# A fused attention and ternary FFN layer on one core: h split one slot later, output scaling on GpSimd, score maxima ahead of gate and up, and weight pieces shared out anew

## What is computed

```python
qkv = x @ Wqkv + bqkv                     # 16 heads of 16, 4 key/value groups
scores = einsum('bqhd,bkhd->bhqk', q, k) / HD
out = softmax(scores) @ v                 # then @ Wout + bout
x = layernorm(x + attention(x))
w_hat = clip(round(w / scale), -1, 1) * scale   # per 64 weights, scale = mean|w|, in bf16
gate, up = split(x @ ternary(w_gate_up).T)      # 1024 each
h = silu(gate) * up
x = layernorm(x + rms_norm(h) @ ternary(w_proj).T)
```

## Time and profile before

| | |
|---|---|
| median of 3 runs | 626.21 us (624.43 to 627.9) |
| the profiled execution: its time, its span | 624.11 us, 622.1 us |
| PE, DVE, ACT, POOL busy | 90%, 74%, 60%, 46% |
| one batch in the loop | 33.3 us |

### The profile page before, as it was taken

How to read it: one execution, slowest core, us unless ns; L and a number is a source line. 1 busy time by engine, 2 the same in 40 slices (tenths; PEclk the granted TensorE clock), 3 DMA queues, 4 the chain that set the end, 5 groups by cost and what they waited for, 6 DMA issues and landing times.

```text
span 622.1 us, 14146 instructions
## 1 busy us (share of the span) xinstructions
PE 556.9 (90%) x4368; PEld 465.6 (75%) x4368; DVE 457.7 (74%) x1066; ACT 373.6 (60%) x738; POOL 288.7 (46%) x404
## 2 busy tenths in 40 slices
PE   5668989999999999999899999999999999899772
PEld 4656768788788787878787877778787877777762
DVE  7785875777877878787878787877878787755753
ACT  4454645666666666757566666666666756575442
POOL 5432331353536353535435453536354535455763
PEclk9697999999999999999999999999999999999996
DMA  7963354444352517061624344352617070101001
GB/s 232 153 131 44 79 86 95 71 95 69 78 104 69 113 45 138 23 136 25 146 35 115 65 98 80 77 102 61 118 43 136 17 144 5 36 3 35 18 0 35
DMA packets 53932, 49.08 MB, mean 79 GB/s; under 512 B 6144, under 2 KB 53888, under 8 KB 53888
## 3 DMA queue, kind: packets, MB, share of 16 engines
q1 hardware_dynamic: 51152, 47.60, 37.1%
q10 hardware_dynamic: 2736, 0.92, 0.6%
HBM read 33.29 MB, written 14.68 MB: 77 GB/s over the span
## 4 chain that ended last, share of the span: by engine, by line
PE 56%; DVE 25%; issue 9%; POOL 4%; ACT 3%; ACTq 2%; DMA 1%; DVEq 0%; POOLq 0%; SPq 0%
PE ffn_ps L447 13%; PE short_ps L447 10%; PE pv_ps L544 8%; PE short_ps L494 6%; PE exp_ps L503 5%; PE down_ps L529 5%; DVE row_max L776 5%; PE short_ps L552 4%; DVE w_hat L809 3%; DVE gated L817 3%; DVE x L880 2%; DVE st L898 2%; DVE h_f L824 2%; DVE r L895 2%; ACTq L746 2%
## 5 line engine op out<-in xcount | busy, mean ns | idle before, releaser
L776 DVE TENSOR_REDUCE row_max<-short_ps 128x2 f32<-128x512 f32 x256 | 173.7, 682 | 47.5 <-PE short_ps L494 47.4
L933 POOL TENSOR_TENSOR h_lo<-h_f,h_hi 128x256 fp32r<-128x256 f32 x128 | 94.8, 740 | 237.5 <-ACT h_hi L672 227.0
L690 ACT ACTIVATE probs<-exp_ps 128x1024 f32<-128x1024 f32 x128 | 130.9, 1023 | 32.7 <-PE exp_ps L503 30.7
L447 PE MATMUL ffn_ps<-x1T_hi,wguT 128*128 128x256 f32 x480 | 125.6, 295 | 21.0 <-DVE x1T_lo L765 10.7
L494 PE MATMUL short_ps<-k_st,q_st 65*128 65x256 f32 x512 | 116.4, 309 | 12.8 <-DVE row_max L776 12.4
L447 PE MATMUL ffn_ps<-x1T_lo,wguT 128*128 128x256 f32 x480 | 118.8, 281 | 0.0
L447 PEld LDWEIGHTS ffn_ps<-x1T_hi,wguT 128*128 128x128 f32 x480 | 90.4, 188 | 30.5 <-DVE h_f L824 13.9
L681 ACT ACTIVATE tanh<-ffn_ps 128x256 f32<-128x256 f32 x120 | 45.8, 381 | 104.3 <-PE ffn_ps L447 83.3
L494 PEld LDWEIGHTS short_ps<-k_st,q_st 65*128 65x128 f32 x512 | 82.1, 192 | 23.7 <-DVE row_max L776 12.3
L447 PEld LDWEIGHTS ffn_ps<-x1T_lo,wguT 128*128 128x128 f32 x480 | 90.5, 189 | 0.0
L938 POOL TENSOR_TENSOR sq_sum<-sq_sum,h_sq 128x256 f32<-128x256 f32 x112 | 82.9, 741 | 0.0
(11 more groups left out here) (98 smaller groups left out, 864.6 us busy)
## 6 DMA issues: line engine op xcount, KB each, us to landing
q_st<-q_dram SPq DMA_DIRECT2D x128, 128.0 KB, 4.1
q_dram<-q_p SPq DMA_DIRECT2D x16, 512.0 KB, 3.0
xn<-in_L_attn_x_dram SPq DMA_DIRECT2D x16, 256.0 KB, 4.6
k_st<-k_dram SPq DMA_DIRECT2D x64, 64.0 KB, 2.3
res<-in_L_attn_x_dram SPq DMA_DIRECT2D x16, 256.0 KB, 3.3
out_dram<-y_out SPq DMA_DIRECT2D x16, 256.0 KB, 2.2
wgu_raw<-in_L_ffn_w_gate_up_dram SPq DMA_DIRECT2D x8, 256.0 KB, 6.5
k_dram<-k_p SPq DMA_DIRECT2D x16, 128.0 KB, 3.1
```

The costliest lines, as they stand in the source:

```text
L447: last = pe.matmul(dst, a, b, start=start and i == 0, stop=stop and i == len(pairs) - 1)
L690: act.activation(probs[:, st.s % 4], exp_ps[:], ACT.Exp).then_inc(exp_done, 1)
L776: dve.tensor_reduce(row_max[:, st.par, head * TT:(head + 1) * TT], short(n, f"max{i}")[:].rearrange("p (t k) -> p t k", t=TT), AX.X, ALU.m ...
L933: pool.tensor_tensor(h_p[1][:, st.s % 4, :], h_f[:, st.s % 2, :], h_p[0][:, st.s % 4, :].bitcast(F32), ALU.subtract).then_inc(h_lo, 1)
```

## The change

Seven edits.

- On PE `gate_up` is issued behind `max_scores(…, 0)` and `exp_scores`, no longer ahead of them. On ACT `exp` goes ahead of `tanh` and of the copy of x.
- `h_hi`, `h_sq` and `h_lo` of a slot's `h_f` are issued one slot later (H_HIGH0, H_LOW0 from 31 to 32), and the sum of squares, its mean and the inverse root move from slot 7 to slot 0 (SUM_SQ, MEAN_SQ, INV from 39 to 40).
- BANK_TABLE changes in slots 0, 1 and 7.
- LN2_APPLY (y_out, two instructions a batch) moves from DVE to POOL.
- `keep_clock` ends at t = 16 and not at 29.
- Pieces 4 to 11 of the weights have their two multiplications on POOL, so that POOL does four instructions for such a piece; `w_hat` has four buffers and not two, `w_scale` two.
- The turns of the pieces follow a table: pieces 1, 2 and 3 are turned at t = 8, 9 and 10, before at 6, 7 and 9; the others as before.

```diff
-SUM_SQ = 39
+SUM_SQ = 40
-H_HIGH0 = 31
-H_LOW0 = 31
-MEAN_SQ = 39
-INV = 39
+H_HIGH0 = 32
+H_LOW0 = 32
+MEAN_SQ = 40
+INV = 40
...
-BANK_TABLE = {0: {"max0": 1, "pv1": 0, "max1": 2},
-              1: {"max0": 1, "x": 2, "max1": 0, "shift1": 1},
+BANK_TABLE = {0: {"max0": 2, "pv1": 0, "max1": 1, "sq": 2},
+              1: {"max0": 1, "x": 0, "max1": 2, "shift1": 1},
...
-              7: {"max0": 2, "v": 0, "max1": 1, "sq": 2}}
+              7: {"max0": 2, "v": 0, "max1": 1}}
...
-W_MAKE, W_TURN, W_PLACE = 1, 4, 5
+W_MAKE = 1
+W_TURN = (5, 8, 9, 10, 12, 14, 16, 18, 20, 22, 24, 26)
-CLOCK_FROM, CLOCK_TO = 2, 30
+CLOCK_FROM, CLOCK_TO = 2, 17
+W_POOL_FROM = 4
...
         @block.tensor
             def slot(n):
-                if st := n.chunk(FFN0):
-                    gate_up(n, st)
                 if st := n.chunk(MAX0):
...
                     exp_scores(st)
                 keep_clock(n, 2)
+                if st := n.chunk(FFN0):
+                    gate_up(n, st)
...
         @block.scalar
             def slot(n):
+                if st := n.chunk(EXP0):
+                    wait(act, exp_scored, st.count(8, st.s + 1))
+                    wait(act, pv_done, st.count(4, st.s // 2 - 1))
+                    act.activation(probs[:, st.s % 4], exp_ps[:], ACT.Exp).then_inc(exp_done, 1)
                 if st := n.chunk(FFN0):
...
-                if st := n.chunk(EXP0):
-                    wait(act, exp_scored, st.count(8, st.s + 1))
...
         @block.vector
+                dve.tensor_tensor(hat, w_abs[:, c % 2], half, ALU.is_gt).then_inc(w_dve, 1)
+                if c < W_POOL_FROM:
+                    dve.wait_ge(w_dve, 3 * c + 1)
+                    dve.tensor_tensor(hat, hat, scale, ALU.mult).then_inc(w_dve, 1)
+                    dve.wait_ge(w_dve, 3 * c + 2)
+                    dve.tensor_tensor(hat, hat, w_sign[:, c % 2], ALU.mult).then_inc(w_dve, 1)
...
-                if st := n.once(LN2_APPLY):
-                    wait(dve, rstd2_done, st.count(1, 1))
...
         @block.gpsimd
+                if st := n.once(LN2_APPLY):
+                    wait(pool, rstd2_done, st.count(1, 1))
+                    wait(pool, stored[st.par], st.count2(16, 0))
...
+                    if c >= W_POOL_FROM:
...
+                        pool.tensor_tensor(hat, hat, scale, ALU.mult).then_inc(w_pool, 1)
+                        pool.wait_ge(w_pool, w_pool_count(c) + 1)
+                        pool.tensor_tensor(hat, hat, w_sign[:, c % 2], ALU.mult).then_inc(w_pool, 1)
```

More of the change, by code:

```diff
@@ L220, in postln_layer @@
         w_sign = sb("w_sign", [P, 2, PG, Q_GROUP], BF16)
-        w_hat = sb("w_hat", [P, 2, PG, Q_GROUP], BF16)
+        w_hat = sb("w_hat", [P, 4, PG, Q_GROUP], BF16)
         w_sum = sb("w_sum", [P, PG])
-        w_scale = sb("w_scale", [P, PG], BF16)
+        w_scale = sb("w_scale", [P, 2, PG], BF16)
         w_half = sb("w_half", [P, PG], BF16)
@@ L359, in piece, with turned_piece, w_dve_count, w_pool_count @@
             return W_READ.index(n.t - later) if n.it is None and n.t - later in W_READ else None
+        def turned_piece(n, later):
+            return W_TURN.index(n.t - later) if n.it is None and n.t - later in W_TURN else None
+        def w_dve_count(c):
+            return 3 * min(c, W_POOL_FROM) + max(c - W_POOL_FROM, 0)
+        def w_pool_count(c):
+            return 2 * min(c, W_POOL_FROM) + 4 * max(c - W_POOL_FROM, 0)
         block = ctx.enter_context(nc.Block())
@@ L563, in keep_clock @@
                     return
-                turned = sum(at + W_TURN < n.t for at in W_READ)
+                turned = sum(at < n.t for at in W_TURN)
                 if turned:
@@ L633, in slot @@
                     turn(bank, [att[:, t, m * P:(m + 1) * P] for m in range(DT) for t in range(TT)], att_turned)
-                if (c := piece(n, W_TURN)) is not None:
+                if (c := turned_piece(n, 0)) is not None:
                     turn_weights(c)
@@ L748, in slot @@
                                 .bitcast(F32), shift_p[half][part][:].bitcast(F32)).then_inc(shift_loaded[half], 16)
-                if (c := piece(n, W_PLACE)) is not None:
+                if (c := turned_piece(n, 1)) is not None:
                     act.wait_ge(w_tr, c + 1)
@@ L794, in tern_weights @@
                 dve.wait_ge(w_red, 3 * c + 1)
-                dve.tensor_scalar(w_scale[:], w_sum[:], 1.0 / Q_GROUP, 1e-8, ALU.mult, ALU.max).then_inc(w_red, 1)
+                dve.tensor_scalar(w_scale[:, c % 2], w_sum[:], 1.0 / Q_GROUP, 1e-8, ALU.mult, ALU.max).then_inc(w_red, 1)
                 dve.wait_ge(w_red, 3 * c + 2)
-                dve.tensor_scalar(w_half[:], w_scale[:], 0.5, None, ALU.mult).then_inc(w_red, 1)
+                dve.tensor_scalar(w_half[:], w_scale[:, c % 2], 0.5, None, ALU.mult).then_inc(w_red, 1)
                 dve.wait_ge(w_red, 3 * c + 3)
-                if c >= 2:
-                    dve.wait_ge(w_tr, c - 1)
+                if c >= 4:
+                    dve.wait_ge(w_tr, c - 3)
                 half = w_half[:].unsqueeze(2).broadcast_to([P, PG, Q_GROUP])
[L802 to L809, removed]
+                scale = w_scale[:, c % 2].unsqueeze(2).broadcast_to([P, PG, Q_GROUP])
+                hat = w_hat[:, c % 4]
+                dve.tensor_tensor(hat, w_abs[:, c % 2], half, ALU.is_gt).then_inc(w_dve, 1)
[4 more added lines that the diff above has]
+                    dve.tensor_tensor(hat, hat, w_sign[:, c % 2], ALU.mult).then_inc(w_dve, 1)
             def slot(n):
@@ L834, in slot @@
                     wait(dve, y_copied, st.count(1, 1))
+                    wait(dve, y_done, st.count(TT, 0))
                     for t in range(TT):
@@ L939, in slot @@
                                            ).then_inc(h_summed, 1)
+                if st := n.once(LN2_APPLY):
+                    wait(pool, rstd2_done, st.count(1, 1))
+                    wait(pool, stored[st.par], st.count2(16, 0))
+                    pool.sem_inc(pool_waited, 1)
+                    for t in range(TT):
+                        pool.tensor_scalar(y_out[:, st.par, t, :], r2[:, t, :], mv2[:, t, 0:1], rstd2[:, t:t + 1],
+                                          ALU.subtract, ALU.mult).then_inc(y_done, 1)
                 if st := n.once(RSTD1):
```

18 lines of the change are left out of this document (9 added, 9 removed).

## The result

| | before | changed |
|---|---|---|
| median | 625.32 us (4 runs, 623.56 to 627.9) | 648.65 us (4 runs, 646.64 to 651.3) |
| ratio | | 1.0372, interval 1.0318 to 1.0427 |
| profiled execution, span | 622.1 | 646.4 |

A forecast was written before the change was run, and what follows sets the result against it. PE was taken as the bound in the batches, with waits for DVE's row maxima in the start. Start -16.4, eleven batches at +1.7 (+18.7) and the rest +3 gave +5.3 on 626.2: 631 us, range 616 to 641.

The forecast's parts named there:

- Slot 0 to 1: Both slots use short1_ps; slot 1's first scores newly wait for slot 0's row maximum, 0.5 us a batch.
- Slot 2 to 3: Both use short0_ps; exp ahead of tanh delays slot 2's maximum, so slot 3's first scores wait: 1.4 us a batch.
- x1T_lo: First scores of slot 7 wait for it in bank 2; the wait of 0.55 us grows by 0.6 a batch.
- h_f: PE's wait for it in slot 5, 0.52 us in the mean, shrinks by 0.4 a batch.
- Shorter DVE blocks and turns: Start: eight pieces lose two DVE instructions each, -7.5 us; first scores no longer queue behind turns of pieces, -1 us.
- Fillers: Start: 26 keep_clock calls of 0.44 us fall away, -11.4 us; waits they covered give back 3.5.
- a rival with a chance of 0.06: Without fillers the start's clock sinks from 0.97 to 0.86, +4 us on 32 of PE's work: 635 us; chance 0.06.
- The prediction's own sign of being wrong: A batch still at 33.4 us, or first gate_up beyond 103 us, the start then held by POOL or the clock.
- The rest: Outside the eleven full batches: the first batch, the last two and the end add +3 us together.
- the order costs little: Rival: maxima end sooner than the chain says, +0.5 us a batch, 616 us in all; chance 0.25.
- a draw: Rival: start -18 us, batches +1.4 us each, 627 us in all; chance 0.22.
- POOL binds the start: Rival: each of eight pieces puts 1.2 us of POOL work on the path, +9.5 us, 641 in all; chance 0.05.

The follow-up runs named there:

- a3: The changed kernel with the three LN2_STATS steps on DVE moved behind the second row maximum of slot 2: 626.53 us, ratio 1.004.
- c_pe: The changed kernel with ACT's old order put back (tanh ahead of exp) and PE's new order kept: 638.44 us, ratio 1.022.
- by: The kernel before with only y_out made on POOL: 623.71 us, ratio 0.997.
- b3: The kernel before with only h_hi, h_sq and h_lo one slot later, their sums moved along, and the matching bank table: 621.22 us, ratio 0.993.
- a2: The changed kernel with the old order put back on PE (gate_up ahead of the scores) and ACT (tanh ahead of exp): 611.33 us, ratio 0.980.
- s30: The kernel before with only the pieces shared out anew (multiplications on POOL, four buffers, turns by the table), fillers kept: 618.55 us, ratio 0.990.
- s17: The kernel before with the pieces shared out anew and without the fillers of t = 17 to 29: 615.68 us, ratio 0.986.
- b4: The kernel before with only the fillers of t = 17 to 29 left out: 623.23 us, ratio 0.997.
- b1: The kernel before with only the new order on PE and ACT: 659.83 us, ratio 1.055.
- a5: The changed kernel with the order of before on PE and ACT and the fillers back up to t = 29: 610.96 us, ratio 0.976.
- a1: The changed kernel, new order kept, with the fillers back up to t = 29: 651.21 us, ratio 1.044.

## Why the prediction was wrong

The direction was right, and so was the mechanism of the waits in the batches. The size was not: +5.3 was forecast, +23 came, and the range ended at 641. Two steps failed: what the fillers give back in the start, and what the order costs outside the eleven full batches.

- **The batches, right as a sum.** Forecast +1.7 a batch and 35.0 us; two batches of the loop take 34.95 in the mean (`probs` at 355.30, 390.06 and 425.20), over all eleven it is +20.3 instead of +18.7, where some of the 1.6 is the spell at the lower clock near 284 us. Slot 0 to 1: forecast 0.5, measured 0.49 to 0.75 by the batch. Slot 2 to 3: 1.4 and 1.17 to 1.36. `x1T_lo`: it was to grow by 0.6 to 1.15 and is about 1.0. `h_f`: it was to shrink by 0.4 and is gone, 0.5. a3 and c_pe confirm two links of the chain of slot 2: LN2_STATS ahead of the maximum, and `exp` ahead of `tanh`.
- **The batches, off in the split.** That the sum is so near is luck in part, since two misses cancel. The order costs 2.40 a batch over the eleven (35.18 against 32.78) where my terms add to 2.1, in all 3.3 us more. The rest of the change gives back 0.56 where I had 0.3, in all 2.9 us: `y_out` was right (by: 0.28), but the later h parts, which I said cost nothing, give 0.47 in b3, with their sums and the table. Of the 2.40, waits are 2.0: from `probs` of t = 39 to that of t = 127 both kernels have 2819 matmuls in the record, with 32.7 us of PE's waits in the changed one and 10.8 in a2. The other 0.4 is busy time, 354.1 against 349.8 us, and my sum had no term for it.
- **The start, the first failed step: the fillers.** Forecast -16.4, bounds -9 and -20; measured -4.2 at t = 31. *Shorter DVE blocks and turns*, -7.5 and -1, were nearly right: s30 has -7.7, and -6.5 by the medians, though its first scores wait 4.3 us for the DMA of q. (The cap that the prediction sets is a little low: from 26 to 110 us PE waits 13.1 us for row maxima before, the 10.9 of the earlier trace rows and 2.2 more at L557.) *Fillers*, -11.4 + 3.5 = -7.9, failed: alone they give 1.8, and beside the pieces another 2 at most (s30 and s17, within the uncertainty). The 11.4 was too large, since calls of 0.44 us overlap the kernel's own matmuls: 8.3 is what went. Of what comes back, the waits were too large with 3.5 (1.6 in b4), and the clock, which took 6.7 in b4, stands at nothing in the sum. I had it as a rival with a chance of 0.06 and let it cost 4 us of 32; the 32 was the same misreading, the work is 39.9 us. The fall to 0.86 that the rival names is what the changed kernel has from 57 to 110 us, b4 has 0.77.
- **The way from -16.4 to -4.2.** `probs` of t = 31 moves by -7.7 with the pieces (s30), +0.2 without fillers (s17), +1.0 with the other edits but the order (a2) and +2.3 with the order. These are single executions. The last step isn't firm: the order moves t = 31 by +1.0 between before and b1 and by -1.0 between a5 and a1, and PE waits for the DMA of the shift row in slot 31 in a2 too, 1.01 us against 2.27. The prediction's own sign of being wrong was there: the first `gate_up` is at 107.78, beyond 103. Of its two reasons the runs point to the clock and not to POOL.
- **The rest, the second failed step.** Forecast +3, measured +2.7 from t = 31 to 39 and +5.6 behind 127, together 8.3. With the old order the two are 0 and -1.5 (32.1 and 109.5), so the order costs 2.8 and 7.1 there. Nearly half of the latter is what a single wait grew by. The first scores of t = 131 wait for the maximum of slot 2, 1.17 us before, 1.16 in a2, and now:

```profile
547.66 0.80 PE L507 MATMUL short_ps<-k_st,q_st 65*128 65x256 f32 x2 [4.38 <-DVE row_max L789]
```

  I had written that slot 2 waits already in the last batches and charged little for it; but a wait that is there already grows by all that the chain behind it grows. A part is busy time at a lower clock. These are the 60 us behind t = 127 in the changed kernel, then in a2, with the same 435 matmuls:

```profile
529.87:591.70 61.83, 54.13 (x435) 44.33 (x434) 39.46 (x97) 34.89 (x70) 31.88 (x45) 0.94 0.08 17
```

```profile
498.40:554.60 56.20, 52.17 (x435) 42.31 (x434) 37.75 (x97) 35.57 (x70) 32.48 (x46) 1.00 0.09 18
```

  Of the 5.6 us between them 2.0 are busy time and 3.7 are waiting.
- The rivals "the order costs little", "a draw" and "POOL binds the start" are out. What the prediction cites on the SBUF interfaces that POOL and DVE share (GPSIMD Engine Reference, the Trainium skill, section 8) may be what shows in `w_half`: 1.12 us where 0.17 is its usual length, twice in twelve, each time beside POOL's addition at L983 and ending within 0.03 us of it. s30, which has one of these, is faster all the same.

The error is 12.2 us of the start, 5.3 of the rest and 1.6 of the batches, together 19.0 ahead of rounding; that is the distance of the profiled difference, 24.3, from 5.3. Told by parts and medians, the order cost 37 us where my terms for it were 23 (eleven times 2.1) and at most the 3 of the rest, and the other parts gave 14 where I had 20.

## What to carry to other kernels

Where an engine is the bound and buffers rotate, the instructions that stand between the last use of a buffer and its next are its slack: walk the chain from the issue to the release on the other engines before that slack is moved, and move a step that nobody waits for behind the one that frees the buffer. Change one engine's order only together with the engine that feeds on it. Filler work of PE can't be subtracted from the time as it stands in a row: take off what overlaps its neighbours, and count what the kernel's own matmuls then cost at a lower clock. The move of LN2_STATS shows that such a price belongs to one order of work: it gave 22 us with the new order and nothing with the old.

## What the runs showed of the hardware

PE's granted clock fell to half, 1.2 GHz, for spells although PE never stood long. In b4 from 57.2 to 110 us it was busy 46.6 of 52.8 us, and its waits made 7.3 us (the one that ends at 57.23 began ahead of the window, so that the idle time inside is 6.2). The longest was the first of these:

```profile
PE short_ps L494 <- DVE row_max L776: 4.4, 4, 1.5
PE short_ps L557 <- DVE row_max L776: 1.3, 2, 0.7
PE exp_ps L503 <- ACT probs L690: 1.0, 2, 0.6
PE short_ps L552 <- ACT q_f L699: 0.6, 1, 0.6
```

The mean clock was 0.77, and for 20 us of the window it was this:

```profile
71.20:91.60 20.40, 18.79 (x95) 12.40 (x99) 15.59 (x36) 10.19 (x15) 8.29 (x8) 0.50 0.54 92
```

At the lower clock PE looks busy, 18.79 of 20.40 us here, so a high busy share is no sign of a full clock. TensorE: Matmul & The Clock Gate (the Trainium skill, Part 1, the second failure mode) tells of a kernel whose many short idles between groups of matmuls make the clock swing; this stretch agrees, with a clock of 1.00 from 57.2 to 71.2 us, 0.50 to 91.6 and 1.00 again to 105.3, and no wait above 1.5 us.

The start shifts by some microseconds with where such spells fall. From 57 to 110 us the mean clock was 1.00 in s30, 0.97 before and 0.87 in b3, which all have the same fillers, and 25 runs of the kernel before took from 621.15 to 629.01 us. A term of the start that is read from one profile is good to a microsecond or two; the medians stand beside it for that.
